# The slots' rows of the third residual and the node network of the graph convolutions as one stage in turn

## The reference, cut to what matters

```python
def _L2_gnn_ref(x, src, dst, Ws, bs, gammas, betas, lin1_w, lin1_b):
    ...
    x_jk = jnp.max(jnp.stack(xs, axis=0), axis=0)
    out = jax.nn.relu(x_jk @ lin1_w + lin1_b)
    return out
def _L3_gnn_ref(x, edge_index, W0, b0, W1, b1, W2, b2):
    ...
    def gcn_layer(h, W, b):
        hW = h @ W
        msg = norm * hW[row]
        out = jax.ops.segment_sum(msg, col, num_segments=N)
        return out + b
    h = jax.nn.relu(gcn_layer(x, W0, b0))
    h = jax.nn.relu(gcn_layer(h, W1, b1))
    h = gcn_layer(h, W2, b2)
    return h
...
x = _layernorm(x + _L2_gnn_ref(x, src, dst, L2_gnn_Ws, ...), axis=-1)
x = _layernorm(x + _L3_gnn_ref(x, edge_index, L3_gnn_W0, ...), axis=-1)
```

## Time and profile before

| what | us |
|---|---|
| median of 3 runs | 7210.41 |
| lowest, highest | 7204.28, 7210.7 |
| the profiled execution's own time | 7209.73 |
| its span, first to last instruction | 7207.8 |

### The profile page before, as it was taken

The page is one execution under the profiler, slowest core; times in us unless marked ns, Lnnn a source line. Parts: engine busy times, 40 slices in busy tenths (PEclk is TensorE's granted clock), DMA queues, the critical chain, the costliest instruction groups (busy, mean ns, idle before and its releaser), DMA issues. The chain is left out here.

```text
span 7207.8 us, 88239 instructions
## 1 busy us (share of the span) xinstructions
...
## 2 busy tenths in 40 slices
...
GB/s 194 277 276 277 214 198 61 126 305 226 245 205 203 195 67 35 175 350 212 140 137 148 129 136 131 122 100 219 270 197 222 222 223 199 209 203 194 95 93 82
DMA packets 1093011, 1317.61 MB, mean 183 GB/s; under 512 B 110351, under 2 KB 791999, under 8 KB 1086254
## 3 DMA queue, kind: packets, MB, share of 16 engines
...
q0 software_dynamic: 117600, 253.84, 17.3%
...
## 5 line engine op out<-in xcount | busy, mean ns | idle before, releaser
L615 POOL DMA_INDIRECT jk_layer_msg<-jk,idx_jk x588 | 591.5, 1006 | 268.2 <-issue 174.0
L615 POOL DMA_INDIRECT gcn_msg<-x,idx x196 | 186.9, 954 | 898.0 <-POOLq L137 838.6
L1148 PE MATMUL jk_layer_sum_ps<-ident,jk_layer_weighted 128*128 128x128 f32 x784 | 185.5, 380 | 540.5 <-ACT jk_layer_weighted L1114 540.5
L1148 PEld LDWEIGHTS jk_layer_sum_ps<-ident,jk_layer_weighted 128*128 128x128 f32 x784 | 118.6, 188 | 660.2 <-ACT jk_layer_weighted L1114 660.2
L742 PE MATMUL gcn_nodes_h_ps<-gcn_nodes_h_t,w_gcn 128*128 128x512 f32 x784 | 352.7, 593 | 0.0
L742 PE MATMUL sage_nodes_h_ps<-sage_nodes_h_t,w_ws 128*128 128x512 f32 x784 | 352.5, 592 | 0.0
L1282 DVE COPY sage_h<-sage_turn 128x512 f32<-128x512 f32 x98 | 67.7, 691 | 417.3 <-PE sage_turn L733 417.3
L615 POOL DMA_INDIRECT sage_small_rows<-meta,src_node x196 | 185.0, 944 | 324.2 <-POOLq L137 264.8
L962 ACT ACTIVATE sage_nodes_h_t<-sage_nodes_h_ps,w_b_c 128x512 f32<-128x512 f32 x392 | 247.8, 683 | 198.8 <-PE sage_nodes_h_ps L742 198.8
L2185 PE MATMUL gcn_end_sum_ps<-ident,gcn_end_rows 128*128 128x128 f32 x196 | 54.6, 434 | 389.4 <-DVE gcn_end_rows L2178 389.4
L615 POOL DMA_INDIRECT sage_end_msg<-h,idx x196 | 197.0, 1005 | 270.2 <-ACT sage_end_weighted L1114 159.5
...
## 6 DMA issues: line engine op xcount, KB each, us to landing
...
```

Of the source, the lines that this page charges most:

```text
L615: pool.indirect_dma_start(out=into[:, g.number % depth, s, :], out_offset=None, in_=table, in_offset=bass.IndirectOffsetOnAxis(ap=index_ti ...
L1148: mm = pe.transpose(ps[:, c, at_s], self.weighted[:, g.b, s, c * P:(c + 1) * P], self.K.ident[:])
```

## The change

The two stages become one, `last_rows_block`. `run_mixed` does what `run_groups` did, but a stage of the list may run at every step (`NODE`) or at every second one (`SLOT`): 98 steps carry a group of nodes each, and every second one a group of slots. A step at which the slots' `make_r` runs is called even here, the other odd.

- PSUM: `bank_x` serves `turn_x` and `make_r`, `bank_y` serves `make_y` and `turn_r`. Before, the slots had two banks for either. So `make_r` waits for the `copy_x` of the same step, and `turn_r` for the `out_y2` of the same step.
- GpSimd adds the lonely row (`add_lonely`, now into a tile of its own, `moved`) and the last bias to `x3` (`add_bias`, into `x3_b`, six deep). DVE then adds `y2` and `x3_b` in one operation (`residual_sum`), and `x3` is not loaded again. DVE's `moments0` is what is left of `add_lonely`.
- One barrier, one filling and one emptying of a pipeline are gone. `last_row` is freed before the stage. The first network's nodes have a function of their own, with the same instructions.

```diff
-def jk_end_block(nc, K, W, tables):
+def run_mixed(eng, stages):
+    low = min(lag for _, lag, _ in stages)
+    most = max(lag for _, lag, _ in stages)
+    for step in range(low, NG + most):
+        for f, lag, every in stages:
+            if 0 <= step - lag < NG and (step - lag) % every == 0:
+                f(Group((step - lag) // every))
+def last_rows_block(nc, K, W, tables, out):
...
+    NODE, SLOT = 1, 2
+    MAKE_R, TURN_R, TURN_X, MAKE_Y = 2, 4, 1, 4
     rows4 = [P, 2, SUB, D]
+    deep = 6
...
+        run_mixed(sp, [(load, -2, NODE), (load_layers, -3, SLOT), (load_slots, 1, SLOT), (store_x3, 2, NODE), (store_h1, 4, NODE),
+                       (store_y2, 5, NODE), (store_slots, 9, SLOT), (store_z, 7, NODE)])
...
+        def add_lonely(g):
+            wait_for(pool, x_loaded, g)
+            wait_for(pool, norm0.done, g.lag(2))
+            pool.tensor_tensor(moved[:, g.b], x_in[:, g.number % 3], to_subs(W.lonely_row), ALU.add).then_inc(lonely_added.sem, 1)
+        def add_bias(g):
+            wait_for(pool, norm0.done, g)
+            wait_for(pool, y_summed, g.lag(deep))
+            pool.tensor_tensor(x3_b[:, g.number % deep], x3[:, g.b], to_subs(W.row["gcn2_b"]), ALU.add).then_inc(x3_biased.sem, 1)
...
+        run_mixed(pool, [(add_lonely, 0, NODE), (add_bias, 2, NODE), (residuals, 8, SLOT)])
...
+        def make_r(g):
             wait_for(pe, maxed, g)
-            wait_for(pe, kept, g.lag(2))
-            layer_t(pe, r_ps[g.b], [(W.m["lin"], top_t[:, g.b])]).then_inc(made.sem, 1)
+            wait_for(pe, x_copied, Group(SLOT * g.number + MAKE_R - TURN_X))
+            wait_for(pe, r_kept, g.lag(1))
+            layer_t(pe, bank_x, [(W.m["lin"], top_t[:, g.b])]).then_inc(r_made.sem, 1)
...
+        def turn_r(g):
+            wait_for(pe, r_kept, g)
+            wait_for(pe, y2_out, Group(SLOT * g.number + TURN_R - MAKE_Y))
+            wait_for(pe, s_added, g.lag(1))
+            turn_back(pe, lanes(bank_y[:, 0, :], D), r_t[:, g.b], range(SUB), K.ident).then_inc(r_turned.sem, 1)
+        run_mixed(pe, [(make_h1, 2, NODE), (turn_x, TURN_X, NODE), (make_r, MAKE_R, SLOT), (make_h2, 3, NODE), (turn_h1, 3, NODE),
+                       (make_y, MAKE_Y, NODE), (turn_r, TURN_R, SLOT)])
...
+        run_mixed(act, [(keep_h1, 2, NODE), (copy_x, TURN_X, NODE), (keep_r, MAKE_R, SLOT), (root(norm0), 0, NODE), (root(norm), 5, NODE),
+                        (root(s_norm), 6, SLOT), (keep_h2, 3, NODE), (out_h1, 3, NODE), (out_y2, MAKE_Y, NODE), (norms, -1, SLOT), (scale, 8, SLOT)])
...
+        def moments0(g):
+            wait_for(dve, lonely_added, g)
+            norm0.vector_moments(dve, g, moved)
...
+        def residual_sum(g):
+            wait_for(dve, y2_out, g)
+            wait_for(dve, x3_biased, g)
+            wait_for(dve, norm.done, g.lag(2))
+            dve.tensor_tensor(y[:, g.b], y2[:, g.b], x3_b[:, g.number % deep], ALU.add).then_inc(y_summed.sem, 1)
+            wait_for(dve, y_summed, g)
+            norm.vector_moments(dve, g, y)
...
+        def add_slots(g):
+            wait_for(dve, r_turned, g)
+            wait_for(dve, s_loaded, g)
+            wait_for(dve, s_norm.done, g.lag(2))
+            dve.tensor_tensor(s_y[:, g.b], lanes(bank_y[:, 0, :], D), s_x[:, g.b], ALU.add).then_inc(s_added.sem, 1)
+            wait_for(dve, s_added, g)
+            s_norm.vector_moments(dve, g, s_y)
...
+        run_mixed(dve, [(apply0, 1, NODE), (add_slots, 5, SLOT), (residual_sum, 5, NODE), (apply, 6, NODE), (apply_slots, 7, SLOT),
+                        (moments0, 0, NODE), (top, 0, SLOT)])
...
-        jk_end_block(nc, K, W, tables)
-        node_net_block(nc, "gcn", K, W, tables, A["x"], out)
+        last_rows_block(nc, K, W, tables, out)
```

More of the change, by code:

```diff
@@ L1001, in root @@
             return lambda g: norm_.scalar_root(act, g, W.eps)
-        stages = [(keep_h1, L + 1), (copy_x, L)]
-        stages += [(out_u, 6), (root(norm), 4), (root(norm2), 5)] if sage else [(root(norm0), 0), (root(norm), 5)]
-        stages += [(keep_h2, L + 2), (out_h1, L + 2), (out_h2 if sage else out_y2, L + 3)] + ([(copy_x1, 5)] if sage else [])
+        stages = [(keep_h1, 1), (copy_x, 0), (out_u, 6), (root(norm), 4), (root(norm2), 5), (keep_h2, 2), (out_h1, 2), (out_h2, 3), (copy_x1, 5)]
         run_groups(act, NG, stages)
@@ L1057, in count_u @@
             ins.then_inc(u_counted.sem, 1)
-        if sage:
-            stages = [(residual, 4), (apply, 5), (second, 5), (apply2, 6), (count_u, 6)]
-        else:
-            stages = [(apply0, 1), (residual, 5), (add_lonely, 0), (apply, 6)]
+        stages = [(residual, 4), (apply, 5), (second, 5), (apply2, 6), (count_u, 6)]
         run_groups(dve, NG, stages)
@@ L2057, in jk_end_block @@
-    pair = S("pair", 2)
+    s_x, s_y, s_z, scaled, residual = (ph.sb(n, rows4) for n in ("s_x", "s_y", "s_z", "scaled", "residual"))
+    bank_x, bank_y = ph.ps("bank_x", [P, 1, GROUP]), ph.ps("bank_y", [P, 1, GROUP])
+    h1_ps, h2_ps = ph.ps("h1_ps", [P, 2, GROUP]), ph.ps("h2_ps", [P, 2, GROUP])
+    ring = ph.ps("ring", [P, SUB, HID])
+    norm0, norm, s_norm = Norm(ph, "norm0", NG), Norm(ph, "norm", NG), Norm(ph, "s_norm", EG)
+    x_loaded, x3_stored, h1_stored, y2_stored, z_stored = A_("x_loaded", 3), A_("x3_stored"), A_("h1_stored"), A_("y2_stored"), A_("z_stored")
@@ L2058, in jk_end_block @@
+    pair = S("pair", EG, 2)
+    r1_rows, y2_rows, x3_rows, x2_rows = (node_rows(tables[n], SLOTS) for n in ("r1", "y2", "x3", "x2"))
     block = ph.block()
@@ L2087, in _, with turn_x @@
     @block.tensor
     def _(pe):
[L2089 to L2098 removed]
+        def turn_x(g):
+            wait_for(pe, norm0.done, g)
+            wait_for(pe, x_copied, g.lag(1))
+            if (g.number + TURN_X - 1 - MAKE_R) % SLOT == 0:
+                wait_for(pe, r_kept, Group((g.number + TURN_X - 1 - MAKE_R) // SLOT))
+            turn_rows(pe, bank_x[:, 0, :], x3[:, g.b], K.ident).then_inc(turned.sem, 1)
@@ new lines, in turn_h1, with make_y @@
+        def turn_h1(g):
+            wait_for(pe, h1_out, g.lag(1))
+            turn_back(pe, ring, h1_t[:, g.b], range(SUB), K.ident).then_inc(h1_turned.sem, 1)
+        def make_y(g):
+            wait_for(pe, h2_kept, g)
+            wait_for(pe, y2_out, g.lag(1))
+            if (g.number + MAKE_Y - 1 - TURN_R) % SLOT == 0:
+                wait_for(pe, s_added, Group((g.number + MAKE_Y - 1 - TURN_R) // SLOT))
+            layer_rows(pe, lanes(bank_y[:, 0, :], D), [(W.m["gcn2"], h2_t[:, g.b])]).then_inc(y_made.sem, 1)
@@ L2100, in _, with copy_x, keep_h1 @@
     @block.scalar
     def _(act):
+        def copy_x(g):
+            wait_for(act, turned, g)
+            wait_for(act, h1_made, g.lag(2))
+            act.copy(x_t[:, g.b, 0, :], bank_x[:, 0, :]).then_inc(x_copied.sem, 1)
+        def keep_h1(g):
+            wait_for(act, h1_made, g)
+            wait_for(act, h2_made, g.lag(2))
+            wait_for(act, h1_turned, g.lag(2))
+            for c in range(2):
+                ins = act.activation(h1_t[:, g.b, c, :], h1_ps[:, c, :], ACT.Relu, bias=W.col["gcn0_b_c"][:, c:c + 1])
+            ins.then_inc(h1_kept.sem, 1)
```

309 lines of the change are left out of this document (147 added, 162 removed).

## The result

The changed kernel takes 7322.18 us (median of 4 runs, 7318.01 to 7326.04), the kernel before 7207.34 beside it (4 runs, 7197.51 to 7210.7): a ratio of 1.0162, 95% interval 1.0144 to 1.0179. It is slower by 115 us. The forecast was 7284 with a range of 7197 to 7350, so the sign and the range held, and the forecast itself was 38 us too low.

What follows compares the result with a forecast made beforehand. A closed path of waits between engines was to bound the joined stage: 24.1 us plus 1.2 for the clock, 25.3 a lap. 41 us and 48 laps make 1255 against 1181.4, +74 on 7209.73: 7284 us, range 7197 to 7350.

Steps and rivals of the forecast that it cites:

- The closed path: Joined stage, `turn_r` through DVE, ACT and PE back to `turn_r`: the least a lap can take, 24.1 us.
- lap: Two steps of nodes and one group of slots: 23.14 us before, 25.3 us forecast.
- The clock: PE slows behind its 4.7 us gap before `make_r`: 1.2 us a lap; rival that it holds, 7227 us, chance 0.18.
- the bound, 1.7 us: Upper end of the clock loss behind PE's gap, from eight records that took 3.68 us instead of 1.99.
- The sum: Joined stage: 41 us and 48 laps of 25.3 us, 1255 us against 1181.4, so +74.
- the ends: Filling and emptying of the joined stage outside its 48 laps: about 41 us.
- Additions on GpSimd off the path: GpSimd's five additions a lap cost nothing; rival that they meet the path, 7337 us, chance 0.05.
- The bound of 1.1: Most that GpSimd's additions add to a lap if one of the five meets the path: 1.1 us.
- DVE's 16.9 us of work: DVE's busy time in a lap after the change, summed from the earlier busy times: 16.9 us.
- Signs named ahead: Trace of the joined stage: waits, a 4 to 5 us gap before `make_r` and clock under 0.98 would show the forecast right.
- The free lap of 17.8 us: PE's work alone, everything hidden: lap 17.8 us, 6924 us; rival that the path does not close, chance 0.12.

Runs made afterwards that it cites:

- E3b: Changed kernel with four weights-only 128x512 matmuls put between `turn_x` and `make_r` in even steps: 7982.89 us, 1.002 times the kernel before.
- E1: Changed kernel with ACT's `norms` one step earlier (lag -2 instead of -1): 7804.54 us, 0.9876 times the kernel before.
- E2: Changed kernel with `moments0` second in DVE's list, ahead of `add_slots`: 7890.51 us, 0.9992 times the kernel before.
- E7: Changed kernel with `make_r` behind `make_h2` in PE's list, bank waits following that order: 7838.33 us, 0.9855 times the kernel before.
- E4: Changed kernel with each of GpSimd's additions done twice: 8020.07 us, 1.0155 times the kernel before.
- E8: Changed kernel with the edits of E1, E2 and E7, and `turn_r` behind the next step's `make_h1`: 7650.53 us, 0.968 times the kernel before.
- E5: Changed kernel with GpSimd's additions moved to DVE: 8135.07 us, 1.0223 times the kernel before.

## Why the prediction was right, and where it was off

- **The closed path: right, every term within 0.25 us.** In the lap shown: `turn_r` to `add_slots` 0.67 (0.7 forecast); `add_slots` to ACT's root 7.58 (7.6); root to `norms` 2.95 (3.2); `norms` to `keep_h1` 2.83 (2.8); `keep_h1` to `make_r` 1.85 (1.75, and 0.1 to start); and at full clock, from E3b, `make_r` 0.94 (0.86) and `make_h2` to `turn_r` 6.98 (6.9, and 0.2 for hand-overs). The sum is 23.80, E3b's lap 23.79, the forecast 24.1. E1, E2 and E7 each took a piece of it away and the lap followed. E4 excludes GpSimd's additions as the bound, and E8 the transfers: it moved 272 GB/s where the changed kernel moves 191.
- **The clock: the right mechanism, the term that was mis-sized.** Forecast 1.2 us a lap, at most 1.7; measured 2.38. The step that failed is the bound, 1.7 us as the most that the gap can cost. The earlier trace rows shows 3.68 us for records that need 1.99, and eight records of the same line take 3.78 at most in the rows around it (6110 to 6190):

```profile
6185.28 3.78 PE L751 MATMUL gcn_h_ps<-w_gcn,gcn_sum_t 128*128 128x256 f32 x8
```

So nearly all of them ran at half clock, there was hardly more to lose in that row, and it could not say what a gap costs that has more work behind it. On the path here stand 4.4 us of work behind the gap, `make_r` and `make_h2`, and the laps lost 1.57, 2.54 and 3.03 us of them. It is not the work behind the gap alone that counts: the same 4.4 us lost 1.7 or nothing behind 2.04 and 3.02 us (E1, E2). Why laps with the same gap lose different amounts, and why 5.16 us (E5) cost less than 4.84, no run here shows.
- **The sum.** 1.18 too little for the clock and 0.3 too much for the path make 0.87 us a lap, 42 us in 48 laps; the ends were 2 us longer. That is the stage's 44 (1299 against 1255). The stages around it took 10.3 us less, what lies outside the spans 0.9 more, and the median lies 4.2 above the profiled execution. That is some 39 above the sum before rounding (7283.3), 38 above 7284.
- **Additions on GpSimd off the path, at nothing: right** (E4), and no application met an addition in the middle of the changed stage: every one of L716 kept its 0.34 us between 5000 and 6100. The bound of 1.1 from the earlier trace rows was sound: 0.88 is what one of them costs where they meet (E8). But DVE's 16.9 us of work already had such a wait in it; it is 16.1. DVE's residual and GpSimd's bias meet in each even step, and there it is GpSimd that takes 1.81 instead of 1.26. The Trainium skill, page SBUF — State Buffer, section "SBUF: two separate sides", says that whoever of the two starts first gets the shared pair for its whole instruction while the other blocks. The traces agree, for an application with one tensor too (2.87 instead of 1.11 in E4), which no row of before had shown.
- **Signs named ahead.** `make_r` 4.84 us behind `turn_x`, L2223 released by PE's transposes, ACT's root waiting some 4 us in odd steps, a clock under 0.98: all there. The distance of two L2223 was to be 24.5 to 26; it was 25.4 to 26.8, so two laps of three lay above it. PE's gap shows "issue" as what ended it, and that it was the copy L2133 follows from its times (5530.47 and 0.61) and from E7, where the same wait names it.
- **What I did not see.** The path was taken as given by the lists, down to `make_r` ahead of `make_h2`. Which of its links are data and which are only order was not asked. Three links, at least, are order: `norms` ahead of `keep_h1` (E1), `moments0` behind the applications (E2), `make_r` ahead of `make_h2` (E7). The free lap of 17.8 us that the prediction gave as out of reach came within 0.6 us (18.43).
